# Pairs of VectorE and ScalarE operations on neighbouring banks made into single operations, in a conditioned linear-attention layer

## The reference, cut to what matters

```python
xn = _ln(x, ln_w, ln_b)
q = xn @ Wq + bq
k = xn @ Wk + bk + (1.0 - src_mask) * -1000000.0
q = softmax(q.reshape(b, t, h, dh), axis=-1)      # over the 32 features of a head
k = softmax(k.reshape(b, t, h, dh), axis=1)       # over the 64 tokens
v = ((xn @ Wv + bv) * src_mask).reshape(b, t, h, dh)
att = einsum('bnhd,bnhl->bhdl', k, v)
y = einsum('bnhd,bhdl->bnhl', q, att).reshape(b, t, d)
scale, shift = split((silu(emb) @ W_emb + b_emb)[:, None, :], 2, axis=2)
hh = _ln(y, ln2_w, ln2_b) * (1.0 + scale) + shift
out = x + silu(hh) @ W_out + b_out
```

## Time and profile before

| | |
|---|---|
| time of three runs | 332.82, 335.39, 336.79 us; median 335.39 |
| the profiled execution | 336.49 us, of which 334.7 us are the span of its instructions |
| busy in the span | PE 315.3 us (94%), DVE 277.3 (83%), POOL 198.3 (59%), ACT 182.7 (55%) |
| chain that ended last | PE 87%, DVE 5%, POOL 3% |
| mean granted TensorE clock | 0.985 |
| DMA | 19.68 MB, about 59 GB/s |

### The profile page before, as it was taken

The page is one execution under the profiler, slowest core; times in us unless marked ns, Lnnn a source line. Parts: engine busy times, 40 slices in busy tenths (PEclk is TensorE's granted clock), DMA queues, the critical chain, the costliest instruction groups (busy, mean ns, idle before and its releaser), DMA issues.

```text
span 334.7 us, 14404 instructions
## 1 busy us (share of the span) xinstructions
PE 315.3 (94%) x5644; PEld 269.0 (80%) x5644; DVE 277.3 (83%) x749; ACT 182.7 (55%) x360; POOL 198.3 (59%) x261
## 2 busy tenths in 40 slices
PE   3999999999999999999999999999999999998736
PEld 1478777988879898988888898989898888988625
DVE  3695888989898989989897979799898989886771
ACT  1327574566484755565574847565556648454240
POOL 2305137767766775767677667757676775747420
PEclk9999999999999999999999999999999999999896
DMA  7702010040404021030304040210304010101011
GB/s 238 256 0 66 20 47 4 2 129 2 127 5 118 7 66 59 11 115 0 125 0 125 0 125 0 71 55 25 101 0 125 0 63 0 66 4 63 4 66 63
DMA packets 19418, 19.68 MB, mean 59 GB/s; under 512 B 817, under 2 KB 18865, under 8 KB 19394
## 3 DMA queue, kind: packets, MB, share of 16 engines
q1 hardware_dynamic: 18144, 17.96, 17.2%
q10 hardware_dynamic: 1250, 1.39, 1.3%
HBM read 10.95 MB, written 8.39 MB: 58 GB/s over the span
## 4 chain that ended last, share of the span: by engine, by line
PE 87%; DVE 5%; POOL 3%; DMA 2%; issue 1%; ACT 1%; SPq 0%; POOLq 0%; DVEq 0%
PE bv L674 29%; PE bk L674 28%; PE by L674 13%; PE by L734 4%; PE by L745 4%; PE by L777 4%; PE by L724 4%; DMA q_t<-in_wv 2%; POOL y_s L350 1%; DVE ystat L647 1%; DVE y_s L640 1%; POOL yr L345 1%; DVE z_s L565 0%; DVE q_s L557 0%; DVE rq L636 0%
## 5 line engine op out<-in xcount | busy, mean ns | idle before, releaser
L408 ACT ACTIVATE k_t<-k_t 128x512 f32<-128x512 f32 x32 | 20.2, 632 | 55.9 <-DVE k_t L591 55.9
L243 POOL TENSOR_TENSOR h_lo<-h_s,h_hi 128x512 fp32r<-128x512 f32 x30 | 38.1, 1290 | 10.0 <-ACT h_hi L434 10.0
L239 POOL TENSOR_TENSOR z_s<-z_s,mod_shift 128x512 f32<-128x512 f32 x30 | 30.7, 1043 | 21.6 <-DVE z_s L565 21.6
L674 PE MATMUL bv<-w_o_hi,h_hi 128*128 128x256 f32 x128 | 35.1, 295 | 4.5 <-ACT h_hi L434 4.5
L358 POOL TENSOR_TENSOR x_all<-x_all,bo_all 128x1024 f32 (+1 forms) x16 | 38.3, 2396 | 0.0
L391 ACT ACTIVATE xt_hi<-by 128x512 fp32r<-128x512 f32 x32 | 17.5, 595 | 37.1 <-PE by L745 37.1
L587 DVE TENSOR_REDUCE kmax<-bk 128x8 f32<-128x512 f32 x32 | 22.0, 687 | 16.2 <-PE bk L674 16.2
L350 POOL TENSOR_SCALAR y_s<-y_s,yr 128x256 f32<-128x256 f32 x62 | 33.8, 558 | 2.6 <-POOL yr L347 2.2
L345 POOL TENSOR_TENSOR yr<-yr,neg_half 128x4 f32<-128x4 f32 x16 | 16.2, 1012 | 31.4 <-DVE yr L654 31.4
L674 PE MATMUL bv<-w_o_lo,h_hi 128*128 128x256 f32 x128 | 34.7, 292 | 0.0
L440 ACT ACTIVATE xhat<-x_all,xr 128x256 f32 (+1 forms) x64 | 33.1, 590 | 2.3 <-POOL xr L333 2.3
(11 more groups left out here) (106 smaller groups left out, 857.6 us busy)
## 6 DMA issues: line engine op xcount, KB each, us to landing
x_all<-in_x SPq DMA_DIRECT2D x16, 512.0 KB, 4.5
out<-x_all SPq DMA_DIRECT2D x15, 512.0 KB, 3.2
z_s<-in_w_emb ACTq DMA_DIRECT2D x1, 512.0 KB, 8.6
h_s<-in_w_emb ACTq DMA_DIRECT2D x1, 512.0 KB, 10.5
out<-x_all SPq DMA_DIRECT2D x2, 256.0 KB, 2.1
y_s<-in_wk SPq DMA_DIRECT2D x1, 256.0 KB, 3.3
q_t<-in_wq SPq DMA_DIRECT2D x1, 256.0 KB, 5.5
th<-in_cond_t ACTq DMA_DIRECT2D x1, 256.0 KB, 7.2
```

The source lines that it names most:

```text
L239: return eng.tensor_tensor(z, z, mod_shift[:, c, span(g, GB)].unsqueeze(2).broadcast_to([P, GB, SEQ]), ALU.add)
L243: return eng.tensor_tensor(h_lo[:, c, :], h_s[:, c, :], h_hi[:, c, :].bitcast(fp32), ALU.subtract)
L408: nc.scalar.activation(k_t[:, par, c, :], k_t[:, par, c, :], ACT.Exp).then_inc(kexp_d, 1)
L674: return nc.tensor.matmul(dst, lhsT, rhs, start=start, stop=stop)
```

## The change

Two operations that did the same work on two neighbouring banks (or on the two halves of an SBUF tile) become one of twice the columns. The PSUM tensors `bk0`, `bk1` and `bv0`, `bv1` become `b_k` and `b_v` of two banks each, and `kv` gets a layout in which the even and the odd sequences are apart, so that one operation can write both. In a full step ScalarE has four operations fewer (`e_k`, exp q, `q_t`, tanh), VectorE seven (two q maxima, two q subtractions, one `rk`, one `kv`, one h). The other pairs (`xt_hi`, `h_hi`, `xt_lo`, z, y, k, residual, v) stay two operations. Each semaphore now counts one where it counted two, and every waiter waits for the whole pair: the q maximum for both v copies, tanh for both halves of z, h for the whole tanh, `h_hi` of either half for the whole of h, the `e_k` copy for both banks of transposes, and `y_transposed` for the whole copy.

```diff
                 if B:
                     g = i - 1
-                    for e in range(2):
-                        wait(act, ekt_d, 2 * g + e + 1)
-                        wait(act, att_d, g)
-                        nc.scalar.activation(e_k[:, 2 * e:2 * e + 2, :].rearrange("p t d -> p (t d)"), be[e][:, :],
-                                             ACT.Copy).then_inc(ek_d, 1)
...
+                    wait(act, ekt_d, 2 * g + 2)
+                    wait(act, att_d, g)
+                    nc.scalar.activation(e_k[:, :, :].rearrange("p t d -> p (t d)"),
+                                         by[:, 0:2, :].rearrange("p e n -> p (e n)"), ACT.Copy).then_inc(ek_d, 1)
...
-                    for c in range(C):
-                        wait(act, z_d, 2 * g + c + 1)
-                        wait(act, h_d, 2 * g)
-                        nc.scalar.activation(th[:, c, :], z_s[:, c, :], ACT.Tanh, scale=0.5).then_inc(th_d, 1)
+                    wait(act, z_d, 2 * g + 2)
+                    wait(act, h_d, g)
+                    nc.scalar.activation(th[:, :, :], z_s[:, :, :], ACT.Tanh, scale=0.5).then_inc(th_d, 1)
...
-                for t in tiles:
-                    wait(dve, v_d, 4 * i + t + 1)
-                    wait(dve, qsub_d, 4 * i + t - 3)
-                    nc.vector.tensor_reduce(out=qmax[:, t, :], in_=q[t], axis=AX.X, op=ALU.max).then_inc(qmax_d, 1)
-                for t in tiles:
...
+                t = tiles[0]
+                pair = slice(t, t + 2)
+                q = (b_v if t == 0 else b_k)[:, :, 0:D].rearrange("p t (h d) -> p t h d", d=DH)
+                wait(dve, v_d, 4 * i + t + 2)
+                wait(dve, qsub_d, 2 * i + t // 2 - 1)
+                nc.vector.tensor_reduce(out=qmax[:, pair, :], in_=q, axis=AX.X, op=ALU.max).then_inc(qmax_d, 1)
+                if t == 0:
+                    wait(dve, eqt_d, 2 * i - 2)
+                wait(dve, qmax_d, 2 * i + t // 2 + 1)
+                nc.vector.tensor_tensor(q_s[:, par, pair, :].rearrange("p t (h d) -> p t h d", d=DH), q,
+                                        qmax[:, pair, :].unsqueeze(3).broadcast_to([P, 2, HEADS, DH]),
+                                        ALU.subtract).then_inc(qsub_d, 1)
...
-                    for c in range(C):
-                        wait(dve, th_d, 2 * g + c + 1)
-                        wait(dve, hlo_d, 2 * g)
-                        nc.vector.scalar_tensor_tensor(h_s[:, c, :], th[:, c, :], 1.0, z_s[:, c, :],
-                                                       ALU.add, ALU.mult).then_inc(h_d, 1)
+                    wait(dve, th_d, g + 1)
+                    wait(dve, hlo_d, 2 * g)
+                    nc.vector.scalar_tensor_tensor(h_s[:, :, :], th[:, :, :], 1.0, z_s[:, :, :],
+                                                   ALU.add, ALU.mult).then_inc(h_d, 1)
```

More of the change, by code:

```diff
@@ L124, in build_layer @@
         bt = [by[:, 2, :], by[:, 3, :]]
-        bk_ = [bank("bk0"), bank("bk1")]
-        bv_ = [bank("bv0"), bank("bv1")]
+        b_k = ctx.enter_context(nc.psum_tensor("b_k", [P, 2, 512], fp32))
+        b_v = ctx.enter_context(nc.psum_tensor("b_v", [P, 2, 512], fp32))
+        bk_ = [b_k[:, 0, :], b_k[:, 1, :]]
+        bv_ = [b_v[:, 0, :], b_v[:, 1, :]]
         bqv = bv_ + bk_
@@ L431, in body @@
                     for c in range(C):
-                        wait(act, h_d, 2 * g + c + 1)
+                        wait(act, h_d, g + 1)
                         wait(act, o_d, 2 * g)
@@ L563, in z_scaled @@
                     wait(dve, yt_d, 2 * g + c + 1)
-                    wait(dve, h_d, 2 * g)
+                    wait(dve, h_d, g)
                     nc.vector.tensor_tensor(
@@ L702, in qv_tile @@
                 if t < 2:
-                    wait(pe, qsub_d, 4 * i + t - 3)
+                    wait(pe, qsub_d, 2 * i - 1)
                     wait(pe, res_d, 2 * (i - 3) + t + 1)
@@ L731, in y_transposed @@
                     if B:
-                        wait(pe, ek_d, 2 * g + c + 3)
+                        wait(pe, ek_d, g + 2)
                     for t in range(T):
@@ L772, in body @@
                     g = i - 1
-                    wait(pe, qexp_d, 2 * g + 2)
+                    wait(pe, qexp_d, g + 1)
                     for c in range(C):
@@ L782, in body @@
                     g = i - 1
-                    wait(pe, ek_d, 2 * g + 2)
+                    wait(pe, ek_d, g + 1)
                     wait(pe, zs_d, 2 * g)
@@ L804, in body @@
                     g = i - 1
-                    wait(pe, kv_d, 2 * g + 2)
-                    wait(pe, qt_d, 2 * g + 2)
+                    wait(pe, kv_d, g + 1)
+                    wait(pe, qt_d, g + 1)
                     for b in range(GB):
@@ L813, in body @@
                                 last = mm(by[e * SEQ:e * SEQ + SEQ, h, col:col + AW],
[L814 removed]
+                                          q_t[rows, c, b * SEQ:b * SEQ + SEQ], kv[rows, e, t, c, :], True, True)
                     last.then_inc(y_d, 1)
@@ L822, in body @@
                     for e in range(2):
-                        wait(pe, qsub_d, 4 * i + e + 1 if F else 4 * G)
+                        wait(pe, qsub_d, 2 * i + 1 if F else 2 * G)
                         if not F:
```

48 lines of the change are left out of this document (18 added, 30 removed).

## The result

| | before | after |
|---|---|---|
| median (lowest to highest) | 335.17 us (332.82 to 337.68, 13 runs) | 337.47 us (335.57 to 340.54, 13 runs) |
| ratio to before | | 1.0066, 95% interval 1.0037 to 1.0096 |
| the profiled execution | 336.49 us, span 334.7 | 337.70 us, span 335.9 |

The change makes the kernel 0.66% slower, 2.2 us (1.2 to 3.2). The interval leaves out no change, and all of it lies within 1%; the forecast was 0.9% slower.

The account below looks back on a forecast made before the run. TensorE was taken to bound the loop, and chains over VectorE, ScalarE and GpSimd the two ends. 0.6 (beginning) + 0.8 (steps 15, 16) + 1.5 (step 17) = +2.9 us, giving 338.3 us; 8-in-10 range 335.4 to 341.1.

Parts of the forecast that it names:

- The loop, nothing: Loop steps: TensorE stays busy for all 18.3 us, so later results on the other engines cost nothing.
- the margin of `e_k`: Loop: fused `e_k` copy ends 0.16 us before `y_transposed` loads its weights, less some 0.06 to hand over; cost nothing.
- VectorE saves 0.22 us a step, worth nothing: `rk`, `kv` and h in each full step: 1.98 us as three operations for 2.20 as six; no time gained.
- The rival that VectorE sets the pace: Loop: VectorE holds TensorE back, so each full step gains 0.22 us, 3.3 us in all, 332.1 us; chance 0.06.
- Durations: Fused operations: VectorE 0.69 us (512 columns), 1.22 (1024); ScalarE 1.03 for a copy, about 1.06 for tanh.
- Beginning, +0.6: Fused q pairs delay `xt_lo` of step 1 and y of step 2, 0.3 us each.
- The waits to look for: Signs of being right: TensorE waits 0.7 us for step 1's `xt_lo` and 0.3 us longer for step 2's y.
- Steps 15 to 17, +0.8: Step 15's y 0.3 us later, step 16's serial tanh, h, `h_hi`, low part; +0.8 us including that 0.3.
- the bounds given: Cost of steps 15 and 16 together: 0.6 to 1.05 us, the upper if TensorE's clock stays low throughout.
- Step 17, +1.5: Step 17: whole tanh, whole h and two `h_hi` in series move TensorE's 325.90 to 327.38, +1.5 us.
- The sum, +2.9: Whole kernel: 0.6 + 0.8 + 1.5 = +2.9 us, or 338.3 us against the median, 0.9% above.
- The rival of the lesser loss: Both ends: only step 17's 1.5 us or less is lost, 335.4 to 336.8 us; chance 0.15.

Follow-up runs that it names:

- q undone: The changed kernel with the q maxima and subtractions as four operations again; ratio to before 1.0126 (1.0089 to 1.0164).

## Why the prediction was right, and where not

- **The loop, nothing:** right. Steps of 18.31 us with TensorE always busy, the margin of `e_k` 0.18 us where 0.16 less the handing over was forecast, and a bracket when the copy is later still.
- **VectorE saves 0.22 us a step, worth nothing:** the worth was right, the size was not. `rk`, `kv` and h took 2.26 us for the 1.98 forecast and the 2.20 of before, since `kv` waits for a longer `rk` to hand over (0.36 us from start to start, where 0.22 was counted). VectorE's busy time fell by 5.2 us in all. The rival that VectorE sets the pace falls: less work on it and an equal step.
- **Durations:** right within 0.02 us, but for `rk`, 0.25 us for 0.19. The q pair took 1.33 us for the 1.34 forecast. The Trainium skill ("VectorE: DVE Perf Modes", The DRAIN you can't avoid) has the next operation wait until the pipe is empty; by that, two operations would have saved some 0.3 us (an estimate), and the trace does not show it, since the four took no longer than the two. The same section adds that an operation that is not held starts earlier, and with that the four overlapping ones agree.
- **Beginning, +0.6:** right, in both halves. From rq to y it is 8.90 to 9.20 us, and 8.90 with q undone. In step 1 `xt_lo` starts 0.34 us later, TensorE's load for it waits for just that, and x transposed to y product is 0.33 us longer; four kernels with q fused and four with q in four operations agree on it. The waits to look for were 0.7 us for `xt_lo`, and there are 0.7 us in two pieces: 0.50 for the q subtraction and 0.20 for `xt_lo`. The first piece is a wait that the prediction had not seen. `b_k` is now counted as a pair, so the product that writes its first bank waits for tile 3's subtraction too. It costs nothing in step 1, because `xt_lo` comes last all the same; step 2 has it too (0.52 us), hidden behind that for y.
- **Steps 15 to 17, +0.8:** it was 0.35 + 0.61 = 0.96, within the bounds given, of which some 0.5 hang on the low clock of the output product, which the upper bound allowed for. The output product did become the last one, as the missing bracket shows. Step 15's part is tied between y and the `e_k` copy, which the prediction had put at nothing there: it had read the copy's margin in the loop alone.
- **Step 17, +1.5:** it was 1.63, shown by doing it alone and by undoing it.
- **The sum, +2.9:** the traces give 3.2, and timing gives 2.2 (1.2 to 3.2). Its terms are all seen in the traces, each within 0.2 us of its forecast; the timing alone could not tell a loss of 1.5 us from one of 3. The forecast lies inside its interval, and the 3.2 us of the traces at its edge. That 2.9 and 2.2 are so near is in part luck, since the stops of TensorE, which were not forecast, differ from kernel to kernel by as much and more. The rival of the lesser loss is not needed, but the interval does not exclude a part of it.

## What to carry to other kernels

Fusing two operations on halves gained nothing here, on engines that don't set the pace (no run has the other case). It takes away a hand-over, and costs at each place where the next engine could have begun on the first half, which is above all where the pipeline fills and drains. There the reverse, halves cut so that the consumer can really start on one, took 0.8 us out of the last step. When buffers are paired, list who waits for the bank to be free as well as who reads the result. And before a difference of 1% is put down to an edit, look in the trace for stops of the bound engine that wait for nothing: they can be larger than the edit's effect.

## What the runs showed that I had not expected

- TensorE stops for 0.2 to 2.5 us though it waits for nothing that the profile shows: 1.75 us at the same product in three runs of two kernels, six products earlier in the kernel with six more ahead, and 31 earlier in step 16 with 32 more. Two kernels became 1.3% slower, over a third of it by such a stop. That an edit to VectorE or ScalarE can move these stops, by way of the waits in TensorE's queue, would fit this and is not shown.
- A product of two columns is not free: 32 took 6.96 us at the start, 0.22 us each, and the loads of their 128x128 weights cover 6.90 us of it.
- One operation of ScalarE or VectorE over two banks costs its columns and no more: 1028 ns for 1024 columns where 512 take 612, the 0.8 ns a column that the smaller operations gave.
